# Splitting a head's maxima into two parts behind the next head's first two maxima, in the 14-wide layers

## The chip, the cores and the metric

The kernel runs on one core of one Trainium2 chip. The metric is the time of one execution on the device in microseconds; the median of three runs of the kernel before is 615.16 us (613.29 to 616.64). Names of engines follow the profile: PE is TensorE, DVE is VectorE, ACT is ScalarE, POOL is GpSimd, SP is SyncE, whose queue issues most transfers.

## The reference, cut to what matters

Three attention blocks and one block in the Fourier domain follow one another on an input of 4 images, 16 by 16 positions, 192 channels. Blocks 0 and 2 attend inside windows 14 wide (12 heads of 16 channels, the image padded to 28 by 28), block 1 attends over the whole image (12 heads of 48 channels). In each block:

```
x   = layernorm(x); q, k, v = x @ w_qkv + b
attn = (q * scale) @ k.T + rel_h[..., None] + rel_w[..., None, :]
attn = softmax(attn)
out  = attn @ v @ w_proj + b_proj
x   = shortcut + out;  x = x + gelu(layernorm(x) @ w1 + b1) @ w2 + b2
```

The softmax needs, for each query of each head, the maximum over its keys. It is this maximum, with its sign turned, that the change is about.

## The kernel before, in words

All products are made in fp32 or in fp32r, a rounded form; an operand that has to keep fp32's precision is therefore held as a high part (rounded) and a low part (what rounding left). For each head h the operands of its scores lie in QA and KA, with the position terms and masks as further rows. They are copied there by three transfers of the SP queue (step `aug`, lines 700 to 733), of which the last one is `QA<-REL`.

Each head goes through these steps, whose order is one list for all engines; every engine walks the list and does its own part of each step (`windowed_attention`, L248, builds it for the 14-wide layers).

- `max`, six units u = 0 to 5 for a head: PE multiplies QA by KA without the row of maxima, into one of two banks in turn (L1218 is the line of all such products); DVE reduces the bank to maxima in NM (L1109). PE may fill a bank again only when the reduction of two units before has left it.
- After the sixth reduction DVE makes the high part (two copies, L1122, 98 rows of 8 and 120 rows of 2 numbers) and the low part (two subtractions, L1126) in HL. Before the copies it waits for its own reduction, before the subtractions for its own copies. NM and HL are double, by the parity of the head.
- `maxT`: PE waits for the low part (`max_lo`), and turns HL with a transpose (L1328). DVE waits for that and copies the result to NR (L1133); SP then issues two transfers of NR into the head's row of QA (L741).
- `scores`, six units: PE makes the scores with that row, ACT takes their exponential (L958).
- `pv` every four heads: the products with V, then `copy_o` on ACT (L978), and two units of `inverse` on DVE (transposes at L1144 and L1146) with `divide` on POOL (L845).

The list runs three heads of maxima ahead of the scores. `maxT` of head h stands directly behind unit 1 of `max` of head h + 1, in every head from 0 to 10; for head 11 it stands behind its own unit 5. So it reads, for the middle of a layer:

```
max6.5 scores4.4 pv4 max7.0 scores4.5 max7.1 maxT6 copy_o0 scores5.0 max7.2 ...
```

The SP queue works its list in order too: the two row transfers of `maxT` of head h stand ahead of `aug` of head h + 3, whose operands `max` of head h + 3 needs. In head 2's stretch POOL splits K of the second chunk of heads (L824, L827, L828), and DVE does the same for Q a little later.

Layer 1 has another list (`whole_attention`) and keeps its code. The change touches only the vector engine's block.

Of the kernel before, what the change touches and what calls it, by code (L numbers as in the profile page):

```python
# [21 lines left out]
F32 = mybir.dt.float32  # L22
F32R = mybir.dt.float32r
ALU = mybir.AluOpType
# [8 lines left out]
HEADS, HALF = 12, 6  # L33
# [5 lines left out]
HALF_IN = INNER // 2  # L39
# [373 lines left out]
def _build(nc, ctx, io, out):  # L413
# [28 lines left out]
    mem = []  # L442
    for L in LAYERS:
        n = L.index
        m = {}
# [554 lines left out]
    def _(dve):  # L1000
        steps = [0]

        def link(ins):
# [2 lines left out]
            ins.then_inc(dve_step, 1)  # L1006
            dve.wait_ge(dve_step, steps[0])

        nc.vector.memset(mem[0]["OT"][:, 0, 0:128], 1.0).then_inc(warm_tile.sem, 1)
        for L, step, i, u, bank in all_steps():  # L1010
            n, m = L.index, mem[L.index]
# [47 lines left out]
            elif step == "split" and u:  # L1059
                dve.wait_ge(*k_done.at(n, 1))  # L1060
                dve.wait_ge(*pad_keys.at(n, 0))
                hi = m["KHL"][:, 0, :]
                nc.vector.tensor_copy(hi, m["k"]).then_inc(k_hi.sem, 1)
                dve.wait_ge(*k_hi.at(n, 0))
                nc.vector.tensor_copy(m["KHL"][:, 1, :], hi.bitcast(F32))
                nc.vector.tensor_tensor(m["KHL"][:, 2, :], m["k"], hi.bitcast(F32), ALU.subtract)\
                    .then_inc(k_lo.sem, 1)
            elif step == "split":
                if i:
                    for wait in chunk_read(L, i - 1):  # L1070
                        dve.wait_ge(*wait)
                dve.wait_ge(*q_done.at(n, 2 * i + 1))
                src = by_place(image(m["q"]))
                hi, lo = by_window(m["QHL"][:, 0, :]), by_window(m["QHL"][:, 1, :])
                for k in range(3):
                    ins = nc.vector.tensor_copy(hi[k], src[k])
                ins.then_inc(q_hi.sem, 1)
                dve.wait_ge(*q_hi.at(n, i))
                nc.vector.tensor_copy(m["QHL"][:, 2, :], m["QHL"][:, 0, :].bitcast(F32))
                for k in range(3):  # L1080
                    ins = nc.vector.tensor_tensor(lo[k], src[k], hi[k].bitcast(F32), ALU.subtract)
                ins.then_inc(q_lo.sem, 1)
            elif step == "k" and u == 0 and L.pads:

                if i:
                    dve.wait_ge(*k_lo.at(n, i - 1))
                nc.vector.tensor_scalar(m["k"][:, FIRST_PAD:FIRST_PAD + PAD_KEYS],
                                        COL[n][0:CK, 8 + L.chunks + i:9 + L.chunks + i].broadcast_to([CK, PAD_KEYS]),
                                        L.scale, None, ALU.mult).then_inc(pad_keys.sem, 1)
            elif step in ("rh", "rw", "rel"):  # L1090

                hi_done, done = {"rh": (rh_hi_done, rh_done), "rw": (rw_hi_done, rw_done),
                                 "rel": (rel_hi_done, rel_done)}[step]
                dve.wait_ge(*hi_done.at(n, 2 * i + u))
                for (lo, src), (hi, _) in zip(rel_views(L, m, step, u, bank, 1), rel_views(L, m, step, u, bank, 0)):
                    ins = nc.vector.tensor_tensor(lo, src, hi.bitcast(F32), ALU.subtract)  # L1096
                ins.then_inc(done.sem, 1)
            elif step == "max":
                h, p, j = i, i % 2, L.max_units * i + u
                dve.wait_ge(*max_psum.at(n, j))  # L1100
                bank, nm = MAX_BANK[j % 2], m["NM"][:, p, :]
                if not L.pads:
                    dst, src = nm[:, 2 * u:2 * u + 2], PS[:, bank, :].rearrange("p (a k) -> p a k", a=2)
                elif u < NB:
                    dst = nm[0:HALF_IN, 2 * u:2 * u + 2]
                    src = PS[0:HALF_IN, bank, 0:2 * INNER].rearrange("p (a k) -> p a k", a=2)
                else:
                    dst, src = nm[0:EDGES, 4 + u:5 + u], PS[0:EDGES, bank, 0:EDGES + PAD_KEYS]
                nc.vector.tensor_reduce(dst, src, AX.X, ALU.max, negate=True).then_inc(max_done.sem, 1)  # L1109
                if u == L.max_units - 1:  # L1110

                    if h == 0:
                        dve.wait_ge(*hl_zero.at(n, 0))
                    elif h >= 2:
                        dve.wait_ge(*maxT_psum.at(n, h - 2))
                    dve.wait_ge(*max_done.at(n, j))
                    hl, inner = m["HL"][:, p, :], HALF_IN if L.pads else 128
                    parts = [(nm[0:inner, 0:8], hl[0:inner, 0:8], hl[0:inner, 8:16])]
                    if L.pads:
                        parts.append((nm[:, 8:10], hl[:, 16:18], hl[:, 18:20]))  # L1120
                    for full, hi, lo in parts:
                        ins = nc.vector.tensor_copy(hi, full)  # L1122
                    ins.then_inc(max_hi.sem, 1)
                    dve.wait_ge(*max_hi.at(n, h))
                    for full, hi, lo in parts:
                        ins = nc.vector.tensor_tensor(lo, full, hi.bitcast(F32), ALU.subtract)  # L1126
                    ins.then_inc(max_lo.sem, 1)
            elif step == "maxT":
                h = i
                dve.wait_ge(*maxT_psum.at(n, h))  # L1130
                if h >= 2:
                    dve.wait_ge(*max_row_at(L, h - 2))
                nc.vector.tensor_copy(m["NR"][:, h % 2, :], PS[0:L.max_cols, TR_BANK, 0:L.max_rows])\  # L1133
                    .then_inc(maxT_done.sem, 1)
            elif step == "inverse":


                if i + u == 0 and L.pads:

                    dve.wait_ge(*k_lo.at(n, L.chunks - 1))  # L1140
                dve.wait_ge(*o_copied.at(n, 2 * i + u))
                turned = m["OT"][:, i, u * 512:(u + 1) * 512]
                inv = m["SUMS"][:, u, 0:16]
                link(nc.vector.transpose(turned, OS[:, u, :]))  # L1144
                link(nc.vector.reciprocal(inv, turned.rearrange("p (b c) -> p b c", c=32)[:, :, L.sum_row]))
                back = nc.vector.transpose(turned, inv.unsqueeze(2).broadcast_to([128, 16, 32]))  # L1146
                if L.pads:
                    back.then_inc(sums_inv.sem, 1)
                else:
                    link(back)  # L1150
                    nc.vector.tensor_tensor(turned, OS[:, u, :], turned, ALU.mult).then_inc(o_done.sem, 1)
            elif step == "norm":

                dve.wait_ge(*pv_done.at(n, HEADS // L.pv_heads * L.pv_steps - 1))
                o = PS[:, O_BANK[i], :]
                turned = m["PT"][:, 0, i * 1024:i * 1024 + 1024] if L.pads else m["PT"][:, i, 0, :]
                sums, rows = turned[:, 0:512].rearrange("p (b c) -> p b c", c=32), turned[:, 512:]
                inv = m["SUMS"][:, 0, i * 16:(i + 1) * 16] if L.pads else m["SUMS"][:, i, 0:16]
                link(nc.vector.transpose(turned[:, 0:512], o))
                link(nc.vector.reciprocal(inv, sums[:, :, L.sum_row]))  # L1160
                link(nc.vector.transpose(rows, inv.unsqueeze(2).broadcast_to([128, 16, 32])))
                pieces = [(m["OT"][:, L.groups - 1, i * 512:(i + 1) * 512], o, rows)]
                if L.pads:
                    pieces = zip(by_place(pieces[0][0].rearrange("p (b y x) -> p b y x", b=2, y=IMG)),
                                 by_window(o, 2), by_window(rows, 2))
                for dst, src, by in pieces:
                    ins = nc.vector.tensor_tensor(dst, src, by, ALU.mult)
                ins.then_inc(o_last.sem, 1)
            elif step == "proj" and u == 1:
                dve.wait_ge(*proj_psum.at(n, i))  # L1170
                nc.vector.tensor_tensor(X[:, i, :], X[:, i, :], PS[:, bank, 0:C], ALU.add).then_inc(x_mid.sem, 1)
            elif step == "down":
                if i % 4 == 0:
                    dve.wait_ge(*x_biased.at(n, i // 4))
                dve.wait_ge(*down_psum.at(n, i))
                nc.vector.tensor_tensor(X[:, i, :], X[:, i, :], PS[:, bank, 0:C], ALU.add).then_inc(x_end.sem, 1)  # L1176
# [375 lines left out]
```

## Time and profile before

| | us |
|---|---|
| median of three runs | 615.16 |
| the profiled execution | 621.33 |
| its span, first to last instruction | 619.5 |
| PE busy in it | 544.5 (88%) |
| DVE busy in it | 303.9 (49%) |
| ACT busy in it | 214.3 (35%) |
| POOL busy in it | 107.6 (17%) |
| mean granted clock of TensorE | 0.932 |

The busy share is a mean over the whole program. Layer 0's heads lie between 34 and 115 us, layer 2's between 430 and 515 us of the span. PE's granted clock has two levels there, 1.00 (2.4 GHz) and 0.50 (1.2 GHz).

### The profile page before, as it was taken

How to read it: one execution, taken by the hardware profiler on the slowest of the kernel's cores; microseconds unless marked ns; L12 is line 12 of the kernel's file. 1: busy time of each engine (PE TensorE's matmuls, PEld its weight loads, DVE VectorE, ACT ScalarE, POOL GpSimd, SP SyncE). 2: the span in 40 equal slices, each digit the busy share in tenths (PEclk: the TensorE clock that was granted, in tenths of full speed). 3: DMA queues.
4: the chain of work that ended last, by engine and by line, in shares of the span. 5: the costliest groups of instructions: out<-in, count | busy, mean ns of one | idle time of the engine just before them, and what ended most of it. 6: DMA issues, size and time to landing. Idle time of an engine off the chain costs nothing.

```text
span 619.5 us, 9854 instructions
## 1 busy us (share of the span) xinstructions
PE 544.5 (88%) x3704; PEld 395.4 (64%) x3704; DVE 303.9 (49%) x822; ACT 214.3 (35%) x425; POOL 107.6 (17%) x169
## 2 busy tenths in 40 slices
PE   7987878789989989998979999989877779899997
PEld 6746766666545756656656956747575557565676
DVE  4758686371221723774756431246774962600143
ACT  4314555432343034433434051341343644222110
POOL 5203010130003403314310061110300110300020
PEclk9999879699989999999999999979967796899999
DMA  5981443514213563473473046016515422200001
GB/s 155 222 202 23 104 93 68 157 46 109 55 39 90 133 153 92 114 173 87 108 184 107 1 105 134 0 33 138 108 27 106 91 42 79 64 1 0 1 1 52
DMA packets 22213, 54.13 MB, mean 87 GB/s; under 512 B 5026, under 2 KB 10906, under 8 KB 22070
## 3 DMA queue, kind: packets, MB, share of 16 engines
q1 hardware_dynamic: 21950, 53.40, 36.1%
q8 instruction: 30, 0.49, 0.4%
q14 instruction: 17, 0.14, 0.1%
q10 hardware_dynamic: 216, 0.10, 0.1%
HBM read 10.94 MB, written 0.79 MB: 19 GB/s over the span
## 4 chain that ended last, share of the span: by engine, by line
PE 63%; DVE 16%; DMA 7%; SPq 5%; issue 4%; ACT 2%; POOL 1%; DVEq 0%; ACTq 0%; POOLq 0%
PE PS L1218 61%; DMA QA<-REL 5%; DVE NM L1109 5%; PE PS L1234 2%; DVE HL L1122 1%; DVE OT L1146 1%; DMA PT<-in_qm 1%; DVE OT L1144 1%; DMA QA<-NR 1%; SPq L667 1%; SPq L733 1%; DVE REL L1096 1%; SPq L668 1%; DVE HL L1126 1%; SPq L718 1%
## 5 line engine op out<-in xcount | busy, mean ns | idle before, releaser
L1109 DVE TENSOR_REDUCE NM<-PS 98x2 f32<-98x392 f32 (+2 forms) x192 | 105.3, 569 | 74.2 <-PE PS L1218 72.4
L958 ACT ACTIVATE PT<-PS 98x392 f32<-98x392 f32 (+2 forms) x192 | 94.0, 521 | 98.5 <-PE PS L1218 94.5
L1218 PE MATMUL PS<-KA,QA 126*98 126x196 f32 (+3 forms) x432 | 97.8, 325 | 28.4 <-DVE NM L1109 17.4
L1218 PEld LDWEIGHTS PS<-KA,QA 126*98 126x98 f32 (+3 forms) x432 | 65.5, 194 | 54.2 <-DVE NM L1109 31.1
L1218 PE MATMUL PS<-QA,KA 128*98 128x196 f32 (+2 forms) x480 | 94.5, 312 | 5.0 <-ACT PT L958 3.2
L1218 PEld LDWEIGHTS PS<-QA,KA 128*98 128x98 f32 (+2 forms) x480 | 74.2, 203 | 14.9 <-ACT PT L958 5.6
L1218 PE MATMUL PS<-XT,WQKV 96*96 96x512 f32 x128 | 64.6, 639 | 5.3 <-issue 4.1
L1218 PE MATMUL PS<-XT,W 96*128 96x512 f32 x144 | 65.2, 607 | 3.4 <-issue 3.4
L1218 PE MATMUL PS<-PT,V 128*32 128x196 f32 (+2 forms) x672 | 54.2, 373 | 0.0
L1218 PE MATMUL PS<-W,HT 128*128 128x192 f32 x288 | 48.7, 328 | 4.7 <-ACT HT L984 4.7
L1218 PEld LDWEIGHTS PS<-W,HT 128*128 128x128 f32 x288 | 46.6, 190 | 9.6 <-ACT HT L984 9.6
L1218 PEld LDWEIGHTS PS<-XT,W 96*128 96x128 f32 x144 | 27.4, 194 | 35.4 <-issue 34.7
L1176 DVE TENSOR_TENSOR X<-X,PS 128x192 f32<-128x192 f32 x24 | 8.5, 354 | 80.0 <-PE PS L1218 80.0
L984 ACT ACTIVATE HT<-PS,COL 128x512 f32<-128x512 f32 x36 | 24.0, 685 | 53.4 <-PE PS L1218 53.4
L1218 PEld LDWEIGHTS PS<-XT,WQKV 96*96 96x96 f32 x128 | 20.9, 174 | 30.7 <-issue 30.7
L1218 PEld LDWEIGHTS PS<-PT,V 128*32 128x32 f32 (+2 forms) x672 | 26.8, 128 | 14.8 <-issue 2.2
L1096 DVE TENSOR_TENSOR REL<-PS,REL 84x64 fp32r<-84x64 f32 (+6 forms) x52 | 20.3, 435 | 29.1 <-ACT REL L929 22.9
L1218 PE MATMUL PS<-WP,OT 128*128 128x192 f32 x192 | 32.0, 328 | 0.0
L1218 PEld LDWEIGHTS PS<-WP,OT 128*128 128x128 f32 x192 | 31.1, 190 | 0.8 <-issue 0.8
L852 POOL TENSOR_TENSOR X<-X,B 128x192 f32<-128x192 f32 x24 | 13.4, 590 | 97.0 <-DVE XNOS L1037 97.0
L845 POOL TENSOR_TENSOR OT<-XNOS,OT 128x512 f32<-128x512 f32 x8 | 10.2, 1269 | 107.8 <-DVE OT L1146 107.8
L895 ACT ACTIVATE XT<-PS,COL 96x512 f32<-96x512 f32 x24 | 17.2, 768 | 26.7 <-PE PS L1234 26.7
(103 smaller groups left out, 657.6 us busy)
## 6 DMA issues: line engine op xcount, KB each, us to landing
QA<-QHL SPq DMA_DIRECT2D x36, 192.0 KB
KA<-KHL SPq DMA_DIRECT2D x24, 228.0 KB
QA<-REL SPq DMA_DIRECT2D x24, 224.0 KB
QA<-QHL SPq DMA_DIRECT2D x12, 384.0 KB
KA<-KHL SPq DMA_DIRECT2D x12, 384.0 KB
KA<-PT SPq DMA_DIRECT2D x12, 380.0 KB
W<-in_w SPq DMA_DIRECT2D x6, 576.0 KB, 5.3
QA<-REL SPq DMA_DIRECT2D x48, 64.0 KB
```

What stands on the lines that cost most here:

```text
L667: sp.dma_start(raw(m["KA"][L.rel_row:L.rows, 0, s, :]), m["KC"]).then_inc(aug_const.sem, 16)
L668: sp.dma_start(raw(m["QA"][L.mask_row:L.max_row, 0, s, :]), m["QM"]).then_inc(aug_const.sem, 16)
L845: nc.gpsimd.tensor_tensor(o, OS[:, k, :], o, ALU.mult).then_inc(o_done.sem, 1)
L852: ins = nc.gpsimd.tensor_tensor(X[:, t, :], X[:, t, :], B2[n][:, :], ALU.add)
L895: nc.scalar.activation(XT[:, k, u * 512:(u + 1) * 512], PS[0:CK, bank + k, :], ACT.Identity, scale=g[:, k:k + 1], bias=g[:, 2 + k:3 + k]). ...
L958: nc.scalar.activation(dst, src, ACT.Exp).then_inc(probs_done.sem, 1)
L984: nc.scalar.activation(m["HT"][:, i, u * 512:(u + 1) * 512], PS[:, bank, :], L.gelu, bias=COL[n][:, b1:b1 + 1]).then_inc(gelu_done.sem, 1)
L1096: ins = nc.vector.tensor_tensor(lo, src, hi.bitcast(F32), ALU.subtract)
L1109: nc.vector.tensor_reduce(dst, src, AX.X, ALU.max, negate=True).then_inc(max_done.sem, 1)
L1176: nc.vector.tensor_tensor(X[:, i, :], X[:, i, :], PS[:, bank, 0:C], ALU.add).then_inc(x_end.sem, 1)
L1218: return nc.tensor.matmul(dst, lhsT, rhs, start=start, stop=stop, skip_group_check=loose)
L1234: last = nc.tensor.transpose(PS[0:CK, bank + k, t * 128:(t + 1) * 128], XN[:, 4 * u + t, k * CK:(k + 1) * CK], IDN[:, :])
```

## The change

The code that made the high and the low part becomes two functions. In layer 1, and for head 11 of the other layers, they are called where they were. In the 14-wide layers the high part of head h is made behind the reduction of unit 0 of head h + 1, the low part behind that of unit 1. The instructions and their waits are the same.

```
+        def high_parts(L, h):
+            n = L.index
+            if h == 0:
+                dve.wait_ge(*hl_zero.at(n, 0))
+            elif h >= 2:
+                dve.wait_ge(*maxT_psum.at(n, h - 2))
+            dve.wait_ge(*max_done.at(n, L.max_units * (h + 1) - 1))
+            for full, hi, lo in max_parts(L, h):
+                ins = nc.vector.tensor_copy(hi, full)
+            ins.then_inc(max_hi.sem, 1)
+        def low_parts(L, h):
+            n = L.index
+            dve.wait_ge(*max_hi.at(n, h))
+            for full, hi, lo in max_parts(L, h):
+                ins = nc.vector.tensor_tensor(lo, full, hi.bitcast(F32), ALU.subtract)
+            ins.then_inc(max_lo.sem, 1)
...
                 nc.vector.tensor_reduce(dst, src, AX.X, ALU.max, negate=True).then_inc(max_done.sem, 1)
-                if u == L.max_units - 1:
...
+                late = L.pads and h + 1 < HEADS
+                if u == L.max_units - 1 and not late:
+                    high_parts(L, h)
+                    low_parts(L, h)
+                if L.pads and h and u < 2:
+                    (high_parts, low_parts)[u](L, h - 1)
```

## Rows read from the trace of the kernel before

**Rows 1.** The page's chain that ended last, shares of the span by engine.
```profile
PE 63%; DVE 16%; DMA 7%; SPq 5%; issue 4%; ACT 2%; POOL 1%; DVEq 0%; ACTq 0%; POOLq 0%
```
**Rows 2.** Waits of PE, whole span: who, for whom, us in total, times, longest.
```profile
PE PS L1328 <- DVE HL L1126: 11.2, 15, 3.0
```
**Rows 3.** Timeline of DVE, heads 0 to 1: start, us, instruction, xcount, [idle before].
```profile
40.24 0.24 DVE L1122 CAST HL<-NM 98x8 fp32r<-98x8 f32 x2
40.52 0.24 DVE L1126 TENSOR_TENSOR HL<-NM,HL 98x8 fp32r<-98x8 f32 x2
40.67 1.03 DVE L1109 TENSOR_REDUCE NM<-PS 98x2 f32<-98x392 f32 x2
```
**Rows 4.** Timeline of layer 0, heads 6 to 9.
```profile
80.33 1.04 DVE L1109 TENSOR_REDUCE NM<-PS 98x2 f32<-98x392 f32 x2 [0.79 <-PE PS L1218]
80.53 0.27 PE L1328 MATMUL PS<-IDN,HL 120*20 120x120 f32 x1
...
81.29 0.26 DVE L1133 CAST NR<-PS 20x120 fp32r<-20x120 f32 x1
...
86.24 1.26 POOL L845 TENSOR_TENSOR OT<-XNOS,OT 128x512 f32<-128x512 f32 x1 [1.21 <-DVE OT L1146]
86.58 0.65 PE L1218 MATMUL PS<-KA,QA 126*98 126x196 f32 x2 [1.29 <-DVE NM L1109]
86.63 0.97 DVE L1122 CAST HL<-NM 98x8 fp32r<-98x8 f32 x2
...
87.93 0.37 PE L1328 MATMUL PS<-IDN,HL 120*20 120x120 f32 x1 [0.70 <-DVE HL L1126]
...
96.14 0.43 PE L1218 MATMUL PS<-KA,QA 126*98 126x196 f32 x2 [1.31 <-DMA QA<-REL]
```
**Rows 5.** Timeline of layer 0, heads 2 to 4.
```profile
50.81 0.65 ACT L938 ACTIVATE REL<-PS 84x448 fp32r<-84x448 f32 x2 [0.42 <-PE PS L1218]
...
52.22 2.78 POOL L828 TENSOR_TENSOR KHL<-OT,KHL 96x1216 fp32r<-96x1216 f32 x1
52.32 0.27 PE L1328 MATMUL PS<-IDN,HL 120*20 120x120 f32 x1 [0.78 <-DVE HL L1126]
...
63.40 0.40 PE L1328 MATMUL PS<-IDN,HL 120*20 120x120 f32 x1
...
64.00 1.02 DVE L1109 TENSOR_REDUCE NM<-PS 98x2 f32<-98x392 f32 x2
...
64.61 0.65 PE L1218 MATMUL PS<-KA,QA 126*98 126x196 f32 x2 [0.48 <-DVE NM L1109]
```
**Rows 6.** Timeline of layer 1, 284 us: a subtraction beside POOL.
```profile
284.11 2.39 POOL L828 TENSOR_TENSOR KHL<-KD,KHL 96x1024 fp32r<-96x1024 f32 x1
284.11 2.40 DVE L1126 TENSOR_TENSOR HL<-NM,HL 128x8 fp32r<-128x8 f32 x1
```
**Rows 7.** Timeline of layer 1, 217 us: a transpose and the copy behind it.
```profile
217.53 0.27 PE L1328 MATMUL PS<-IDN,HL 128*16 128x128 f32 x1 [1.61 <-DVE V L1052]
...
217.84 0.28 DVE L1133 CAST NR<-PS 16x128 fp32r<-16x128 f32 x1 [0.45 <-PE PS L1328]
```
**Rows 8.** Timeline of PE at head 6's first maximum, layer 0, layer 2.
```profile
72.15 0.42 PE L1218 MATMUL PS<-KA,QA 126*98 126x196 f32 x2 [1.11 <-DMA QA<-REL]
...
469.55 0.48 PE L1218 MATMUL PS<-KA,QA 126*98 126x196 f32 x1 [3.33 <-DMA QA<-REL]
```
**Rows 9.** Windows of layer 0: stretch, us, busy by engine (instructions), PEclk, DMA share, GB/s.
```profile
80.50:87.90 7.40, 4.11 (x26) 2.87 (x24) 7.13 (x18) 4.26 (x13) 2.54 (x2) 0.81 0.42 89
87.90:92.20 4.30, 4.27 (x24) 4.18 (x24) 3.75 (x12) 2.38 (x6) 0.00 (x0) 0.53 0.16 48
92.20:96.80 4.60, 3.25 (x24) 2.68 (x24) 3.64 (x12) 2.85 (x6) 0.00 (x0) 1.00 0.74 159
...
96.80:104.50 7.70, 7.70 (x137) 5.48 (x136) 3.76 (x12) 2.92 (x6) 0.00 (x0) 1.00 0.33 60
```
**Rows 10.** Chain of waits, layer 0, head 10: start, us, what.
```profile
105.82 0.72 DVE OT L1144
```

More of the change, by code:

```diff
@@ L1007, in link, with max_parts @@
             dve.wait_ge(dve_step, steps[0])
+        def max_parts(L, h):
+            m = mem[L.index]
+            nm, hl, inner = m["NM"][:, h % 2, :], m["HL"][:, h % 2, :], HALF_IN if L.pads else 128
+            parts = [(nm[0:inner, 0:8], hl[0:inner, 0:8], hl[0:inner, 8:16])]
+            if L.pads:
+                parts.append((nm[:, 8:10], hl[:, 16:18], hl[:, 18:20]))
+            return parts
+        def high_parts(L, h):
[14 more added lines that the diff above has]
+            ins.then_inc(max_lo.sem, 1)
         nc.vector.memset(mem[0]["OT"][:, 0, 0:128], 1.0).then_inc(warm_tile.sem, 1)
@@ L1109, in _ @@
                 nc.vector.tensor_reduce(dst, src, AX.X, ALU.max, negate=True).then_inc(max_done.sem, 1)
-                if u == L.max_units - 1:
[L1112 to L1127, printed above, removed]
+                late = L.pads and h + 1 < HEADS
[4 more added lines that the diff above has]
+                    (high_parts, low_parts)[u](L, h - 1)
             elif step == "maxT":
```

## The prediction

> **What bounds the kernel now.** I read the page's chain first: 63% of the span runs through PE and 16% through DVE [rows 1], so a wait put on PE is paid unless something later was going to wait anyway. Then the waits of PE: it has waited for the low part at its transpose 15 times of 36, 11.2 us in all [rows 2]. Then the timeline at a head's border. In head 6 PE makes the product of unit 1 of head 7 and goes on to the transpose of head 6 at 80.53 with no wait; the two reductions of head 7 run on DVE only from 80.33 to 81.37 [rows 4]. So the low part has been ready before PE comes to it, and that slack is what the change spends. Last the windows: from 80.50 to 87.90 DVE is busy 7.13 of 7.40 us, so there the chain is DVE's; from 92.20 to 96.80 PE waits for a transfer, and from 96.80 to 104.50 PE is busy all of 7.70 us [rows 9]. The three kinds of stretch pay differently.
>
> **What the change adds.** No instruction is added or removed. But PE's list has the transpose of head h directly behind its own product for unit 1 of head h + 1, and the low part now comes behind DVE's reduction of that same product. PE waits at the transpose for product, reduction and two subtractions, every time, 22 times in the two layers. Queued behind it on PE are the scores of the head three back and the next maxima; ACT's exponentials wait for the former, DVE's for the latter; on DVE the copy to NR waits for the transpose and SP's row transfers behind that.
>
> Step by step for one border. A reduction lets the next one start 0.48 us after its own start: two take 1.03, one 0.55 [rows 3]. The pair of copies holds DVE about 0.16 of its 0.24 us span, as the pair of subtractions does (40.52 to the reduction at 40.67, [rows 3]). So from the start of the first reduction: 0.48 to the copies, 0.16 to the second reduction, 0.48 to the subtractions, 0.23 for these, and 0.06 until PE starts (head 7's copies end at 87.60, 0.04 and 0.23 later its subtractions, and the transpose starts at 87.93 [rows 4]): 1.41 us. Head 6: 80.33 + 1.41 = 81.74 against 80.53 [rows 4], so PE stalls 1.21 us. The copy to NR starts 0.31 us behind a transpose when DVE is waiting for it [rows 7], at 82.05 against 81.29.
>
> What DVE gains: before, its copies start 0.10 us behind the end of the sixth reduction, and the subtractions 0.04 behind the copies, where unwaited instructions overlap by 0.08; these two bubbles, some 0.3 us a head, go. It is in the 1.41 already. The Trainium skill speaks against this term ("VectorE: DVE Perf Modes", The DRAIN you can't avoid): chained operations of VectorE pay the same pipeline flush with or without a semaphore between them, so taking apart the dependent pairs would gain nothing. By that page each border would be some 0.2 us dearer and the total some 4 us higher; the overlap of the reductions in the rows says otherwise for instructions that need not wait.
>
> Now border by border, since what follows decides:
> - Heads 0 and 1 (products and reductions take turns). In head 0 the first reduction moves up from 40.67 to about 40.07, by the 0.60 us that the four small instructions held it [rows 3]; 40.07 + 1.41 = 41.48 against a transpose at 40.52 + 0.24 + 0.05 = 40.81, so 0.67 late, of which some 0.2 was a wait for DVE anyway. I take 1.2 us for both heads.
> - Head 2. The copies get into POOL's way. ACT has the high part of the position terms at 51.46, DVE needs 0.7 us for them, the first reduction comes at 52.17 and the copies at 52.65, when POOL has begun its subtraction of K, 52.22 to 55.00 [rows 5]. A subtraction of DVE beside such an instruction took 2.40 us, as long as POOL's own 2.39 [rows 6], and a pair of copies beside POOL's multiply 0.97 instead of 0.24, until POOL had ended at 87.50 [rows 4]. So the copies wait until 55.0, and the transpose comes at 55.0 + 0.16 + 0.48 + 0.23 + 0.06 = 55.94 against 52.32 [rows 5]: 3.6 us. What follows is DVE's work for the second chunk, fed by PE, with nothing to take it back. If POOL did not hold it: 52.17 + 1.41 = 53.58, 1.3 us. I take 3.6, since both rows of such a meeting show it whole.
> - Head 3. The reductions start at 64.00 because DVE has other work; 65.41 against 63.40 is 2.0 us late [rows 5]. PE's next maximum waited 0.48 for DVE anyway: 1.5 us.
> - Head 4: between head 0 and head 6, 0.95 us.
> - But heads 3 and 4 run into the wait for head 6's operands, 1.11 us in layer 0 and 3.33 in layer 2 [rows 8]. Its transfers stand behind head 3's row transfers on SP, which are late only by NR's shift, 65.41 + 0.31 against 64.95, where its reductions let it start (64.00 + 1.02 - 0.08) [rows 5], 0.8 us. PE is late by 1.5 + 0.95 = 2.45. Left over: 2.45 - 1.11 = 1.35 in layer 0, and 0.8 in layer 2.
> - Head 5, before the long PE stretch, and head 9 likewise [rows 9]: 1.2 us each, nothing takes it back.
> - Head 6: DVE's chain follows. Its next reduction needs PE's product behind the transpose: 1.1 us.
> - Heads 7 and 8: head 7's copies meet POOL's multiply already; now they would wait till 87.50 with the first reduction done before. 87.51 + 0.16 + 0.48 + 0.23 + 0.06 = 88.44 against 87.93 [rows 4]: 0.5, and 0.95 for head 8. The wait of 1.31 us for head 10's operands [rows 4] absorbs this but for 0.15, since NR of head 7, which its transfers follow, hardly moves.
> - Head 10: DVE waited until 105.82 for ACT's copy [rows 10], which the transpose doesn't hold; NR would be done at 106.24: 0.4 us.
> Head 11 and layer 1 keep their code: 0.
>
> Layer 0: 1.2 + 3.6 + 1.35 + 1.2 + 1.1 + 0.15 + 1.2 + 0.4 = 10.2. Layer 2, whose trace repeats this some 395 us later: 10.2 - 0.55 = 9.65. Together 19.8 us.
>
> **The clock.** From 87.90 to 92.20 PE had 0.53 of its clock; in the stretch before, where the clock fell (its mean is 0.81), PE was busy only 4.11 of 7.40 us, with a wait of 1.29 us near its end [rows 4, 9]. That head took 4.30 us; the next, at 1.00, 4.60 with 1.31 of waiting, so 3.29 of work [rows 9]. A head at the low level so costs 1.0 us, or 0.23 of its time, where PE bounds. Stalls of 1.2 us at each border are of the size before which it fell. Bounds: 0, and all that is at 1.00 and PE's in the two layers, twice two stretches of 7.7 and two heads of 3.3, 44 us, of which 0.23 is 10 us. I take 4, four heads' worth, in the long PE stretches above all. The Trainium skill's rule ("TensorE: Matmul & The Clock Gate", What's actually happening) has the clock fall only after an idle stretch of the engine, not after a busy one with short waits; by it this term would be 0. The row of 0.53 behind waits of about a microsecond is against it.
>
> Sum: 19.8 + 4 = 23.8. The profiled execution took 621.33, so 645 in its own terms; it lies 1.0% above the median of the runs, and the sum of waits doesn't scale with that. From the median, 615.16 + 23.8 = 639 us.
>
> **Rivals.**
> A, held copies don't happen and the clock doesn't move: head 2 costs 1.3 in each layer, 19.8 - 4.6 = 15.2, so 630 us. For it: the meeting with POOL hangs on 0.4 us (52.65 against 52.22). Against it: POOL starts on its own events, earlier than DVE can come.
> B, the clock falls in most of both layers: 19.8 + 10, and stalls of DVE's chain growing with slower products by 0.1 each, 2 more: 647 us. For it: the border stalls come every 4.4 us. Against: from 92.20 to 96.80 PE waited 1.31 us and kept 1.00, before and after [rows 9].
> C, not slower: DVE's chain is what counts and PE's stall is taken back at its next wait for DVE. Then only the freed bubbles are left, 0.3 us in the 10 borders (heads 0, 1, 2, 6, 10 of both layers) where DVE's chain follows: 3 us faster, 612. It decides if PE's stall of 1.2 is smaller than what PE waits for DVE behind it. [rows 9] has 3.3 us of idle PE in 80.50 to 87.90 that could take it, but the reductions there need the products behind the stalled transpose, and in 96.80 to 104.50 there is no idle PE at all.
> D, the transpose doesn't wait as I say, because the waits of 11.2 us [rows 2] were mostly this already and only change place: 615, no change. The 15 waits of 36 leave 21 transposes without one, which speaks against it.
>
> **Chances.** Forecast 0.56, A 0.18, B 0.20, C 0.03, D 0.03. The forecast's own range is 634 to 643. The range that holds 8 in 10 goes from A's lower side to B's upper: 627 to 650. About 0.5% (3 us) is what a measurement of this kernel can tell; faster 0.03, same 0.03, slower 0.94.
>
> **What would show it.** In the profile after, all 22 transposes in layers 0 and 2 but head 11's wait for DVE, 1.0 to 2.0 us each, and in head 2 about 3.5; the wait for `QA<-REL` at head 6 and head 10 is gone in layer 0 and down to about 1.7 at head 6 in layer 2. The copies of head 2 show 2 us or more beside POOL. The stretch from head 5's transpose to head 6's stays 7.7 us if the clock holds and grows to 9 if not. The forecast is wrong if the transposes wait under 0.5 us, if head 2's copies take 0.24 us, or if the mean granted clock falls below 0.90.

## The result: slower, 637 us against 615, and the profile after

The changed kernel takes 636.97 us (median of four, 633.52 to 639.38), the kernel before in the same runs 614.59: 1.032 of it, 95% interval 1.025 to 1.038, or 22.4 us more. The forecast was 639, from a sum of 23.8. Here and below, ratios and their intervals leave out executions in the chip's occasional slower state, which the medians keep.

The page after gives the chain that ended last like this, shares by engine, to set beside [rows 1]:

```profile
PE 65%; DVE 14%; issue 6%; DMA 6%; SPq 5%; ACT 2%; POOL 1%; DVEq 0%; ACTq 0%
```

PE's waits over the whole span after (who, for whom, us in total, times, longest). The first line answers to [rows 2]: 15 waits and 11.2 us have become 30 and 34.6. The second is PE's wait for a head's operands.

```profile
PE PS L1347 <- DVE HL L1035: 34.6, 30, 3.1
...
PE PS L1237 <- DMA QA<-REL: 3.5, 3, 2.7
```

That second wait was 10.4 us in 7 waits before. PE also waits less for DVE's reductions, 11.5 us where it was 17.4.

The same border as in [rows 4], head 6 of layer 0, on DVE (start, us, instruction, xcount, idle before):

```profile
92.78 0.57 DVE L1138 TENSOR_REDUCE NM<-PS 98x2 f32<-98x392 f32 x1 [1.41 <-PE PS L1237]
93.26 0.23 DVE L1027 CAST HL<-NM 98x8 fp32r<-98x8 f32 x2
93.40 0.56 DVE L1138 TENSOR_REDUCE NM<-PS 98x2 f32<-98x392 f32 x1
93.87 0.23 DVE L1035 TENSOR_TENSOR HL<-NM,HL 98x8 fp32r<-98x8 f32 x2
94.47 0.27 DVE L1152 CAST NR<-PS 20x120 fp32r<-20x120 f32 x1 [0.36 <-PE PS L1347]
```

and on PE:

```profile
92.80 0.34 PE L1237 MATMUL PS<-KA,QA 126*98 126x196 f32 x2
94.16 0.27 PE L1347 MATMUL PS<-IDN,HL 120*20 120x120 f32 x1 [1.02 <-DVE HL L1035]
```

Reduction, copies, reduction, subtractions follow one another without a bubble, as the change meant; and PE stands still for 1.02 us. From the first reduction to the transpose are 94.16 - 92.78 = 1.38 us; the forecast had 1.41. The copy to NR follows the transpose by 0.31.

Head 2, to set beside [rows 5]:

```profile
57.91 2.75 POOL L828 TENSOR_TENSOR KHL<-OT,KHL 96x1216 fp32r<-96x1216 f32 x1
...
58.94 0.55 DVE L1138 TENSOR_REDUCE NM<-PS 98x2 f32<-98x392 f32 x1
59.42 1.35 DVE L1027 CAST HL<-NM 98x8 fp32r<-98x8 f32 x2
60.68 0.55 DVE L1138 TENSOR_REDUCE NM<-PS 98x2 f32<-98x392 f32 x1
61.16 0.22 DVE L1035 TENSOR_TENSOR HL<-NM,HL 98x8 fp32r<-98x8 f32 x2
61.43 0.27 PE L1347 MATMUL PS<-IDN,HL 120*20 120x120 f32 x1 [3.12 <-DVE HL L1035]
```

The copies end only when POOL's subtraction has ended, at 57.91 + 2.75 = 60.66, and PE waits 3.12 us. The wait for head 6's operands, 1.11 in [rows 8], is 0.19:

```profile
83.39 0.42 PE L1237 MATMUL PS<-KA,QA 126*98 126x196 f32 x2 [0.19 <-DMA QA<-REL]
```

The heads of layer 0 and of layer 2, each from the first maximum of head 1 to the transpose of head 11 (stretch, us, busy time and instructions of PE, PEld, DVE, ACT and POOL, granted clock of PE, DMA share, GB/s). Before:

```profile
39.50:111.90 72.40, 56.20 (x538) 44.12 (x537) 55.48 (x156) 34.61 (x86) 10.25 (x7) 0.89 0.37 81
434.50:511.30 76.80, 58.96 (x538) 46.31 (x536) 55.12 (x156) 34.53 (x86) 10.22 (x7) 0.83 0.34 73
```

After:

```profile
45.40:127.30 81.90, 59.99 (x539) 48.27 (x537) 54.09 (x156) 34.95 (x86) 10.23 (x7) 0.79 0.28 61
446.60:529.30 82.70, 61.10 (x539) 49.42 (x537) 54.08 (x156) 34.94 (x86) 10.19 (x7) 0.79 0.32 68
```

DVE is busy 1.0 to 1.4 us less in each layer, the freed bubbles and overlaps; the layers are 9.5 and 5.9 us longer, and the clock is lower. PE is busy 5.9 us more in the two with the same instructions, at the lower clock, and idle 9.5 us more. The windows of layer 2 compare badly, since the profiled execution of before had an unusual wait of 3.33 us there [rows 8] and a low clock behind it. The same code of layer 2 took 72.60 us in experiment 11, which makes its loss 10.1. The span grew by 18.0 us only: besides the heads, 6.0 were lost ahead of head 1 of layer 0 (2.2 of them to a transfer at the start, the rest at a clock of 0.51 behind it, where before had 1.00), and 3.2 came back between the layers, where the code is the same. Such differences come and go between executions, and the sum is better checked in the heads than in one span.

### The profile page after: what moved, and what is told of

It is laid out like the page before. It is cut to its first block, busy times and chain, and to the rows that moved or that the text cites. A ratio compares the mean times of both kernels' runs of the same rounds, so it can differ in the third digit from the quotient of the medians.

```text
span 637.5 us, 9854 instructions
## 1 busy us (share of the span) xinstructions
PE 552.4 (87%) x3704; PEld 404.2 (63%) x3704; DVE 299.8 (47%) x822; ACT 215.3 (34%) x425; POOL 107.9 (17%) x169
## 4 chain that ended last, share of the span: by engine, by line
PE 65%; DVE 14%; issue 6%; DMA 6%; SPq 5%; ACT 2%; POOL 1%; DVEq 0%; ACTq 0%
PE PS L1237 62%; DVE NM L1138 4%; DMA QA<-REL 3%; PE PS L1253 2%; DVE HL L1027 1%; PE PS L1347 1%; SPq L733 1%; DMA PT<-in_qm 1%; DMA QA<-NR 1%; SPq L667 1%; DVE HL L1035 1%; DVE OT L1165 1%; SPq L668 1%; DVE OT L1163 1%; ACT REL L938 1%
## 5 line engine op out<-in xcount | busy, mean ns | idle before, releaser
L1138 DVE TENSOR_REDUCE NM<-PS 98x2 f32<-98x392 f32 (+2 forms) x192 | 107.1, 571 | 82.7 <-PE PS L1237 80.4
L1237 PE MATMUL PS<-KA,QA 126*98 126x196 f32 (+3 forms) x432 | 102.3, 339 | 15.9 <-DVE NM L1138 11.5
L1237 PE MATMUL PS<-QA,KA 128*98 128x196 f32 (+2 forms) x480 | 99.1, 324 | 3.8 <-DMA QA<-NR 2.8
L1237 PEld LDWEIGHTS PS<-KA,QA 126*98 126x98 f32 (+3 forms) x432 | 71.1, 210 | 39.7 <-DVE NM L1138 22.0
L1237 PEld LDWEIGHTS PS<-QA,KA 128*98 128x98 f32 (+2 forms) x480 | 79.3, 216 | 13.1 <-issue 5.4
L1237 PEld LDWEIGHTS PS<-XT,W 96*128 96x128 f32 x144 | 27.4, 194 | 35.4 <-issue 34.6
L1347 PE MATMUL PS<-IDN,HL 120*20 120x120 f32 (+1 forms) x36 | 10.8, 300 | 39.0 <-DVE HL L1035 34.6
L1125 DVE TENSOR_TENSOR REL<-PS,REL 84x64 fp32r<-84x64 f32 (+6 forms) x52 | 20.3, 435 | 37.0 <-ACT REL L929 21.5
L1347 PEld LDWEIGHTS PS<-IDN,HL 120*20 120x20 f32 (+1 forms) x36 | 3.2, 89 | 48.2 <-DVE HL L1035 42.6
L845 POOL TENSOR_TENSOR OT<-XNOS,OT 128x512 f32<-128x512 f32 x8 | 10.2, 1270 | 123.2 <-DVE OT L1165 123.2
```

The source lines that it names most:

```text
L845: nc.gpsimd.tensor_tensor(o, OS[:, k, :], o, ALU.mult).then_inc(o_done.sem, 1)
L1237: return nc.tensor.matmul(dst, lhsT, rhs, start=start, stop=stop, skip_group_check=loose)
L1347: nc.tensor.transpose(PS[0:L.max_cols, TR_BANK, 0:L.max_rows], m["HL"][:, h % 2, :].bitcast(F32), IDN[0:L.max_rows, 0:L.max_rows]).then_in ...
```

## The experiments

The runs came in three jobs, each on another chip: experiments 1 to 4, 5 to 8, and 9 to 11. In these the median of the kernel before was 619 to 621 us, not 615, and single executions of one kernel lay up to 3.6% apart, so each kernel is read as a ratio to before in its own job, and the traces are read beside it. In the first job, and for experiment 11, the difference of the medians is smaller than the ratio says; the ratio decides.

**1. The wait alone.** The kernel before, with one more wait on PE:

```
                 pe.wait_ge(*max_lo.at(n, h))
+                if L.pads and h + 1 < HEADS:
+                    pe.wait_ge(*max_done.at(n, L.max_units * (h + 1) + 1))
```

> The kernel before, its vector code untouched; only PE's transpose of head h (14-wide layers, heads 0 to 10) waits in addition for the reduction of unit 1 of head h + 1. Theory (PE's place in the list: the transpose has to wait for a reduction of the next head): transposes stall 0.9 us at a normal border (80.53 to the reduction's end 81.37 + 0.06), 1.5 at head 2 and 3, part of it taken back in the waits for operands of heads 6 and 10: 6 to 7 us a layer, so 627 to 629 us, well over half of the change's 22. Rival (what costs is on DVE: copies held beside POOL and the new order of small instructions): near the kernel before, 614 to 617 us.

Measured: 635.94 us against a median of 621.32 for before, 14.6 more; the ratio is 1.032 (1.021 to 1.042), or 19.6 us, against 1.032 for the change. The border of head 6, with DVE's order as it was (the extra wait shows as "issue"):

```profile
94.32 1.04 DVE L1109 TENSOR_REDUCE NM<-PS 98x2 f32<-98x392 f32 x2 [0.79 <-PE PS L1218]
94.34 0.34 PE L1218 MATMUL PS<-KA,QA 126*98 126x196 f32 x2
95.46 0.26 PE L1330 MATMUL PS<-IDN,HL 120*20 120x120 f32 x1 [0.78 <-issue]
```

The rival, that DVE's new order costs, falls: with the vector code untouched most of the loss is there, 13 to 26 us by the interval. The theory's 12 to 14 us is at the lower end. Whether the wait alone costs all of the change's 22 us or some 60% of it can't be told from these; that it is the larger part can. The waits of DVE for POOL in head 2 are not all the change's own either: here, with DVE's old order, its subtractions met POOL's and took 2.6 us in layer 0, and PE waited 3.01 us.

**2. Both parts behind unit 0.**

```
-                if L.pads and h and u < 2:
-                    (high_parts, low_parts)[u](L, h - 1)
+                if L.pads and h and u == 0:
+                    high_parts(L, h - 1)
+                    low_parts(L, h - 1)
```

> The changed kernel, but high and low part of head h are both made behind unit 0 of head h + 1, before the reduction of unit 1. Theory: the transpose no longer waits for the second product and its reduction, but still for the first reduction and four small instructions: from its start 0.48 + 0.24 + 0.04 + 0.23 + 0.06 = 1.05 us instead of 1.41, so stalls of 0.85 instead of 1.2; head 2's copies are still held by POOL. 0.3 us less at 22 borders less what was absorbed anyway: 630 to 634 us. Rival (only the wait for unit 1's reduction counts): 615 to 620 us. Rival (the clock's fall counts most and comes with any stall): 636 us.

Measured: 631.14 us, ratio 1.024 (1.013 to 1.036), 8 to 22 us over before. Head 6's transpose:

```profile
89.34 0.57 DVE L1138 TENSOR_REDUCE NM<-PS 98x2 f32<-98x392 f32 x1 [1.41 <-PE PS L1238]
...
89.83 0.23 DVE L1027 CAST HL<-NM 98x8 fp32r<-98x8 f32 x2
...
90.09 0.24 DVE L1035 TENSOR_TENSOR HL<-NM,HL 98x8 fp32r<-98x8 f32 x2
...
90.39 0.27 PE L1348 MATMUL PS<-IDN,HL 120*20 120x120 f32 x1 [0.68 <-DVE HL L1035]
```

1.05 us from the reduction's start to the transpose, as worked out. Set against the 615 us that the expectations go by, the ratio is the lower end of the theory's range (1.024 to 1.031) and above the first rival's (1.008); the second rival (636, 1.034) is inside the interval, so the experiment doesn't decide against it.

**3. Head 2 as before.** The two conditions get `and h != 2` and `and h != 3`.

> The changed kernel, with head 2's parts of both 14-wide layers back behind its own sixth reduction. Theory: head 2's border, where the copies run into POOL's subtraction, costs 3.6 us in each layer, 2.3 until the transpose and 1.2 behind it with PE at the low clock; put back it gives 6 to 7 us: 630 us. Rival (that border is like the others, and the held copies had slack): 1.2 us in each layer, 634 to 635 us.

Measured: 635.19 us, ratio 1.031 (1.021 to 1.041), no gain over the change's 1.032 that can be told. The theory had 6 to 7 us, 1.024; the rival's time, 1.031 to 1.033, is what was measured. Layer 2, head 2:

```profile
455.86 1.28 DVE L1027 CAST HL<-NM 98x8 fp32r<-98x8 f32 x2
455.88 1.23 POOL L827 CAST KHL<-KHL 96x1216 fp32r<-96x1216 f32 x1
457.08 2.75 POOL L828 TENSOR_TENSOR KHL<-OT,KHL 96x1216 fp32r<-96x1216 f32 x1
457.17 2.75 DVE L1035 TENSOR_TENSOR HL<-NM,HL 98x8 fp32r<-98x8 f32 x2
...
459.98 0.27 PE L1347 MATMUL PS<-IDN,HL 120*20 120x120 f32 x1 [2.43 <-DVE HL L1035]
```

In layer 2 the subtractions, in their old place, now meet POOL's long subtraction, since the stalls of heads 0 and 1 have made DVE late against POOL: the experiment moved the collision. In layer 0 it took it away: the transpose didn't wait at all. Yet from head 2's first maximum to head 4's that layer still took 20.8 us, where before took 17.5 and the change 21.7, and PE's granted clock was 0.50 from 54.20 to 67.50. So the held copies are not what most of this border costs, in line with the rival; see the account of head 2 below.

**4. The transpose one unit later, with the change.** The list puts `maxT` behind unit 2 of the next head:

```
-        if j % L.max_units == 1 and j > L.max_units:
+        if j % L.max_units == 2 and j > L.max_units:
...
-                if turned < ahead + (taken - 2) // L.max_units:
+                if turned < ahead + (taken - 3) // L.max_units:
```

> The changed kernel, with the transpose of head h one place later in the list of all engines, behind unit 2 of head h + 1 instead of unit 1. Theory: PE has one product and one unit of scores more, 0.75 us, before it waits: stalls of 1.0 fall to about 0.3, head 2 stays at 2 to 3; NR and the transfers behind it come no earlier. 22 us of loss fall to 6 to 10: 621 to 625 us. Rival (the waits on DVE and POOL cost, wherever PE stands): 634 to 637 us. Second rival (the later row transfers push the operands of heads 6 and 10 so far that the gain is lost there): 632 us, with waits of 2 us for QA<-REL.

Measured: 629.42 us, 8.1 over before's median, ratio 1.013 (0.993 to 1.033), which is -4 to 20 us. PE's waits at the transpose fell by half, those for operands grew (whole span):

```profile
PE PS L1347 <- DVE HL L1035: 17.8, 21, 3.0
...
PE PS L1237 <- DMA QA<-REL: 6.5, 4, 2.0
```

Half of the stall goes, and 8 us of the loss remain by the medians, as the theory had it. The interval is too wide to rule out the second rival's 632 us (1.028), whose waits of 2 us for operands the trace does have; the first rival's 634 us (1.031) lies near its end. Experiment 6 shows what the 8 us may be.

**5. The change once more.**

> The changed kernel itself once more, beside the others of this job, since the chip of the first four runs gave 621 us for the kernel before and not 615. Theory: about 22 us over the kernel before of this job, 1.035 of it. If it lies at 1.025 or less, the four runs before are to be read against a smaller loss.

Measured: 640.58 us, 1.036 (1.031 to 1.041), 21.4 us over the 619.21 of its job. The loss is the same on this chip. Its trace is a second execution of the changed kernel, used below to see what varies.

**6. The transpose one unit later, without the change.** The edit of experiment 4 on the kernel before.

> The kernel before, with the transpose of head h one place later, behind unit 2 of head h + 1: the control for the changed kernel with that same move. The parts have long been made, so no transpose waits; but NR and SP's transfers come 0.75 us later, in front of the operands of heads 6 and 10. Theory: those two waits grow by 0.75 each in each layer, 3 us at most: 615 to 618 on a chip where before is 615. Rival (the move itself costs as much as the changed kernel kept with it, 8 us): 623 us.

Measured: 629.88 us, 1.018 (1.012 to 1.024). The theory of 1 to 3 us falls and the rival stands: the move alone costs 10.7 us by the medians (8 to 15 by the interval), as much as experiment 4 kept. The two profiled executions have the same span, 626.5 us, and the heads of the two layers take 158.0 us in experiment 4 and 156.7 here, so with the transpose behind unit 2 the late parts cost about 1 us in the traces; the times of two jobs can't tell it better than to some 10 us. No transpose but head 11's waits in the two layers' heads, but others do (layer 0, 35 to 124 us):

```profile
PE PS L1218 <- DVE NM L1109: 10.8, 12, 4.0
PE PS L1218 <- DMA QA<-REL: 5.6, 3, 2.2
```

Before these were 8.0 and 2.8 us in nearly the same stretch, which leaves part of the loss unexplained. One piece I can name: head 10's operands come late, PE waits 1.80 us, and runs the head with `pv` behind it at a mean clock of 0.81, 9.2 us from head 10's to head 11's first maximum instead of 7.7. The same 1.5 us show at heads 6 and 10 of layer 2 (set against the unchanged layer 2 of experiment 11). The rest stays open.

**7. Products in the wait.** The changed kernel, with PE busy while it waits:

```
+                claim(TR_BANK, maxT_done.at(n, h))
+                if L.pads and h + 1 < HEADS:
+                    for _ in range(4):
+                        mm(PS[:, TR_BANK, 256:384], IDN[:, :], IDN[:, :], True, True)
                 pe.wait_ge(*max_lo.at(n, h))
-                claim(TR_BANK, maxT_done.at(n, h))
```

`claim` waits until the bank is free; it moved up because the added products write to that bank.

> The changed kernel, with four products of 128 x 128 by 128 on PE (their result is not used) in front of each transpose's wait in the 14-wide layers, heads 0 to 10: 0.9 us at the high level, inside stalls of 1.0 us and more, so that PE is busy while it waits. It tells the clock's part of the loss from the waits'. Theory of the forecast (the stalls lower the granted clock and that costs about 4 us): the clock in the two layers' heads rises from 0.76 to 0.87 or more and the kernel gets 3 to 5 us faster, 632 us. Rival (clock and time are nearly apart, since what runs at the low level lies beside other waits): the clock rises and the time stays within 1 us. If the products overrun the stall at the low level (1.8 us instead of 0.9), it is slower by up to 0.8 us at each such border.

Measured: 636.53 us, 1.027 (1.020 to 1.035), against 640.58 and 1.036 (1.031 to 1.041) for the change in the same job. The windows of the two layers' heads in this kernel, then in the changed kernel of the same job (experiment 5):

```profile
40.30:122.50 82.20, 68.47 (x626) 56.24 (x625) 54.54 (x156) 34.48 (x86) 10.21 (x7) 0.86 0.33 70
443.60:524.80 81.20, 68.16 (x626) 56.03 (x624) 53.64 (x156) 34.42 (x86) 10.21 (x7) 0.86 0.31 70
```

```profile
39.20:124.60 85.40, 63.65 (x540) 49.86 (x538) 52.80 (x156) 34.78 (x86) 10.24 (x7) 0.78 0.31 68
447.10:530.60 83.50, 62.09 (x539) 50.80 (x537) 54.22 (x156) 35.20 (x86) 10.19 (x7) 0.78 0.32 68
```

Most transposes come as late behind their products as in the change, 1.38 us; at head 7 of both layers the added products overrun the wait and make it 2.33 instead of 1.82. The clock is 0.86 against 0.78, and the heads are 3.2 and 2.3 us shorter though 88 products were added. But the profiled execution of this kernel, 631.80 us, was one of its fastest, and that of experiment 5, 640.71, was at its median. Against the first profile of the changed kernel (81.90 and 82.70 us) the heads are only 1.2 us shorter in all. By the medians it is 4.0 us, and the intervals of the two ratios overlap. A gain from the clock is likely; its size is between 1 and 5.5 us in these traces. And 17 of the 22 us stay with the clock at 0.86.

**8. POOL behind head 2.** The changed kernel, with one more wait before POOL's split of K:

```
                     pool.wait_ge(*pad_keys.at(n, i))
+                    pool.wait_ge(*max_lo.at(n, 2))
```

> The changed kernel, with POOL's split of K for the second chunk waiting until the low part of head 2 is made, so that nothing of POOL lies beside head 2's copies. Theory (POOL holds the copies until its subtraction ends): the pair of copies falls from 1.35 to 0.24 us, the stall of head 2's transpose from 3.1 to 1.3 to 1.9 us, and with less of the low clock behind it 2 to 3 us a layer go: 631 to 633 us where the changed kernel has 637. Rival (the stall of head 2 is the wait for the position terms from ACT): the stall stays above 2.5 us and the time where it was.

Measured: 636.79 us, 1.030 (1.024 to 1.036), 3.8 us less than the change in its job. Head 2 of layer 0:

```profile
56.05 0.23 DVE L1028 CAST HL<-NM 98x8 fp32r<-98x8 f32 x2
...
56.94 0.37 PE L1348 MATMUL PS<-IDN,HL 120*20 120x120 f32 x1 [1.37 <-DVE HL L1036]
57.05 1.19 POOL L825 CAST KHL<-OT 96x1216 fp32r<-96x1216 f32 x1 [36.03 <-DVE HL L1036]
```

The copies take 0.23 us, where the first profile of the change had 1.35, and the transpose waits 1.37 instead of 3.12. But the changed kernel as it is sometimes escapes the hold. In the profile of experiment 5, layer 0, POOL's subtraction had started at 51.72 and was ending when the copies came:

```profile
51.72 2.77 POOL L828 TENSOR_TENSOR KHL<-OT,KHL 96x1216 fp32r<-96x1216 f32 x1
54.28 0.30 DVE L1027 CAST HL<-NM 98x8 fp32r<-98x8 f32 x2
55.25 0.37 PE L1347 MATMUL PS<-IDN,HL 120*20 120x120 f32 x1 [1.45 <-DVE HL L1035]
```

So POOL's hold is real, 1 to 2 us of the transpose's wait. What it costs the kernel is little: from head 2's first maximum to head 4's, experiment 8 took 22.4 and 21.5 us in its two layers, experiment 5 22.4 (no hold) and 22.3 (held). The theory's 2 to 3 us a layer came only in part, 0.8 us in layer 2; the 3.8 us by the medians are inside the two intervals together.

**9 and 10. The kernel before, with the remedies of 8 and 7.** In 9 the wait of experiment 8; in 10 four unused products before the first maximum of heads 6 and 10, ten before the transpose of head 11.

> The kernel before, with POOL's split of K for the second chunk waiting for head 2's low part. Theory: the copies and subtractions of head 2 fall from 1.2 us a pair to 0.24, so the transpose's wait of 0.3 to 0.8 us goes; but POOL's work then ends at about 56 us, beside the copies of Q's split on DVE from 56 us on, which it holds for up to 1 us. Together no more than 1 us either way: the same as before. If it were clearly faster, POOL's hold would have been worth removing in the kernel before already.

> The kernel before, with unused products on PE in front of waits that it has anyway in the 14-wide layers: four before the first maximum of heads 6 and 10, ten before the transpose of head 11. Theory (the granted clock falls after such waits, and what follows at the low level costs): the low stretches at 85, 109 and 484, 508 us shrink or go, mean clock from 0.93 to 0.95, and 3 to 5 us less than the kernel before of this job. Rival: the clock rises and the time doesn't move, or the products overrun the waits and it is 1 us slower.

Measured: 619.22 us, 1.002 (0.998 to 1.007), and 619.07 us, 0.998 (0.994 to 1.003), against 619.83 for before. Neither is faster by an amount that can be told. In 10 the granted clock, as a mean over all its executions, is 0.942, where before's is 0.929 in the same job, and the medians are 0.8 us apart; the expected gain of 3 to 5 us didn't come (the interval reaches from 4 us faster to 1.7 slower).

**11. Layer 0 alone.** `late` and the calls hold for `L.index == 0` only.

> The change in layer 0 alone. Theory: both layers carry their own half of the loss and nothing is given back between them: half of the changed kernel's 22 us, 11 us over the kernel before of this job, 1.018 of it. Rival (the delay of layer 0 is partly taken back in layer 1, where transfers are prefetched): under 7 us.

Measured: 630.53 us, 1.024 (1.017 to 1.030), which is 14.6 us, 10.6 to 18.6 by the interval, and 10.7 us by the medians; the theory had 11 (1.018). Its two layers, changed and unchanged in one execution:

```profile
43.90:127.90 84.00, 62.68 (x538) 49.61 (x536) 53.00 (x156) 34.70 (x86) 10.22 (x7) 0.78 0.28 60
450.40:523.00 72.60, 56.88 (x539) 45.14 (x537) 55.02 (x156) 34.61 (x86) 10.20 (x7) 0.87 0.37 78
```

The two layers have the same list of heads; with the change it takes 11.4 us longer. The rival (under 7 us) is out: the loss of layer 0 is not taken back in layer 1.

## Why the prediction was right, step by step

**The stall.** Right in mechanism and size: 1.38 for 1.41 us from reduction to transpose at a normal border. All 22 transposes wait, 0.8 to 1.1 us at the normal borders, 1.77 at head 3. Experiment 1 makes most of the loss with the wait alone. The waits at the transpose trebled, so the rival that they only change place is out; PE's waits for DVE's reductions fell by 5.9 us, so a part of the stall was taken back, but far from all of it, and the rival that built on this (612 us) is out too.

**Border by border.** Taking each first maximum's delay in the profile after against before, the borders of layer 0 cost: heads 0 and 1 together 0.8 (forecast 1.2), head 2 3.6 (3.6), heads 3 and 4 0.9 (1.35), head 5 1.2 (1.2), head 6 1.2 (1.1), heads 7 and 8 0.2 (0.15), head 9 1.2 (1.2), head 10 0.4 (0.4): 9.4 for 10.2. So the waits for the operands of heads 6 and 10 did absorb what was in front of them, and did all but vanish. Layer 2 gives 4.0, 1.2, 0.2, 1.4 and 0.4 for heads 2, 6, 7 and 8, 9, and 10; its heads 3 to 5 can't be compared, because of the 3.33 us wait and the low clock of that one execution before. The forecast took that wait as a rule for layer 2 and expected 1.7 us of it to be left; it was 0.07 after. In experiment 11, whose layer 2 has the old code, it was 1.11 as in layer 0, so the smaller sum for layer 2 (9.65) rested on one unusual wait; against that execution the layer lost 10.1.

**Head 2.** The 3.6 us came out, but not for the reason given, and that is luck. I had POOL's subtraction run until the same moment relative to DVE's work. It came 1.1 us earlier against head 3's first maximum; POOL's first cast in front of it is released by a transfer (`QA<-REL`) in both profiles, not by DVE's small instructions. So the transpose's wait grew by 2.3 us, not 3.6. The other 1.2 us came behind it: from the transpose to head 4's first maximum PE was at the low clock. Before (51.50 to 62.20, of which 0.8 lie ahead of the transpose) and after (61.40 to 72.60):

```profile
51.50:62.20 10.70, 7.21 (x70) 7.00 (x70) 9.03 (x27) 4.84 (x14) 3.45 (x2) 0.95 0.01 2
```

```profile
61.40:72.60 11.20, 10.17 (x70) 9.93 (x70) 6.27 (x17) 4.40 (x12) 0.00 (x0) 0.54 0.01 1
```

The same 70 instructions keep PE busy 10.17 us instead of 7.21. And in experiment 5, layer 0, where the copies were not held and the transpose waited 1.45 us, the stretch behind it was longer still:

```profile
55.20:67.10 11.90, 10.86 (x70) 10.62 (x70) 6.27 (x17) 4.39 (x12) 0.00 (x0) 0.50 0.01 1
```

From head 2's first maximum to head 4's it is 17.5 us before, 21.7 in the first profile of the change with the copies held, 22.4 in experiment 5 and 22.4 in the changed layer of experiment 11 without the hold. So what this part of the layer loses, some 4 to 5 us, doesn't hang on POOL's hold; in each of these PE ran the stretch behind the transpose at 0.50 to 0.54. Rival A, which priced the border at 1.3 us if the hold didn't happen, had this wrong as well. Nor was such a hold new: before, head 2's copies and subtractions took over a microsecond each beside POOL's two casts (49.72 to 52.18), where they take 0.24 elsewhere [rows 3]:

```profile
49.84 1.16 DVE L1122 CAST HL<-NM 98x8 fp32r<-98x8 f32 x2
51.04 1.22 DVE L1126 TENSOR_TENSOR HL<-NM,HL 98x8 fp32r<-98x8 f32 x2
```

**The clock.** I put it at 4 us, against a rule of the Trainium skill ("TensorE: Matmul & The Clock Gate", What's actually happening) that would have made it 0, because the stalls are short and PE is busy between them. The granted clock in the heads fell from 0.89 and 0.83 to 0.79, and experiment 7, with PE kept busy in the waits, gives back 1 to 5.5 us, so the row was the better guide and the 4 is within what was seen. But the sum's two terms can't be checked one by one: the 9.4 and 10.1 us of the borders already hold what the lower clock cost there, and no second 4 us was found in the heads. With experiment 11's layer 2 as the measure of before, the heads lost 19.6 us, 8.0 of them as longer products and 11.6 as idle time of PE. The forecast's 23.8 against a measured 22.4 is closer than its parts are. My place for it was wrong in the profile after: the stretch of products with V behind head 5 kept its clock and its 7.10 us:

```profile
85.20:92.30 7.10, 7.07 (x129) 4.88 (x129) 2.37 (x5) 1.99 (x4) 0.00 (x0) 1.00 0.75 151
```

In experiment 5 the same stretch lost the clock in part, and took 8.60:

```profile
79.90:88.50 8.60, 8.56 (x129) 5.46 (x129) 2.37 (x5) 1.99 (x4) 0.00 (x0) 0.80 0.58 118
```

So this term differs from one execution to the next of the same kernel, which is part of their spread.

**The gain on DVE.** 2.4 us of DVE's busy time in the two layers, and the pairs no longer wait for each other: the first reduction and the copies now overlap. The other rule I weighed (the Trainium skill, "VectorE: DVE Perf Modes", The DRAIN you can't avoid) would have had no such gain, as I read it; but the same section also says that a next instruction which is not held starts earlier. With copies starting 0.48 us behind the start of a reduction of 0.57, the trace agrees with that sentence and with the rows. The kernel got no faster by it.

## What to carry to other kernels

Before moving a step later on one engine, look at who is queued to wait for it and where that engine's list puts the wait: here DVE had the slack, PE did not, and 0.1 us of DVE's busy time saved at each border (2.4 over 22) cost about 1 us of PE. Add up such stalls only up to the next wait that was there anyway, and then look at what the engine's clock does behind them. A wait put on the bounding engine, alone, is a cheap experiment: it showed the larger part of the loss with two added lines. And look at a second execution of the same kernel before a collision in one trace is given a price.

## What the runs showed of the hardware that I had not expected

A small instruction of DVE can take far longer beside one of POOL: in experiment 3 a pair of subtractions, 98 rows of 8 numbers and 120 rows of 2, took 2.75 us instead of 0.23, with the order of both engines unchanged there, because stalls elsewhere had shifted one against the other. PE's granted clock stayed at 0.50 through 11.9 us of which PE was busy 10.86 (experiment 5, behind head 2's transpose). And a higher mean clock didn't buy time in the kernel before (0.942 against 0.929, medians 619.07 and 619.83 us); in the changed kernel 0.86 against 0.78 in the heads went with 2 to 3 us a layer against one execution, and with 1.2 us in both layers together against another at 0.79.
